# One-hot lookups turned round: the one-hot stationary, 512 table columns moving, seven tables and no pairs of tiles

## The reference

```python
e = jnp.stack([tbl_0[ids[:, 0]], ..., tbl_31[ids[:, 31]]], axis=1)      # (2048, 32, 256)
z = einsum('bnd,bmd->bnm', e, e)[:, iu, ju]                             # (2048, 496), i < j
h = concatenate([z, dense_ctx], axis=1)                                 # (2048, 512)
h = maximum(h @ W_top1 + b_top1, 0)                                     # 512
h = maximum(h @ W_top2 + b_top2, 0)                                     # 256
y = h @ W_top3                                                          # (2048, 1)
```

## Time and profile before

| | |
|---|---|
| median of 3 runs | 572.25 us (570.58 to 574.01) |
| the profiled execution | 570.71 us |
| its span | 568.9 us |
| TensorE matmul busy | 520.8 us (92%) |
| TensorE weight load busy | 472.5 us (83%) |
| ScalarE busy | 413.4 us (73%) |
| GpSimd busy | 405.4 us (71%) |
| VectorE busy | 129.8 us (23%) |

### The profile page before, as it was taken

The page is one execution under the profiler, slowest core; times in us unless marked ns, Lnnn a source line. Parts: engine busy times, 40 slices in busy tenths (PEclk is TensorE's granted clock), DMA queues, the critical chain, the costliest instruction groups (busy, mean ns, idle before and its releaser), DMA issues.

```text
span 568.9 us, 24720 instructions
## 1 busy us (share of the span) xinstructions
PE 520.8 (92%) x11291; PEld 472.5 (83%) x11291; DVE 129.8 (23%) x201; ACT 413.4 (73%) x743; POOL 405.4 (71%) x426
## 2 busy tenths in 40 slices
PE   0766999999999989999899999989999999999797
PEld 0656989999999989898789989989998999999655
DVE  1345031311304040312204040310404031220401
ACT  3968687878878778877678787867877887663502
POOL 6778777777777777777777777777777777777400
PEclk9977899999999999999999999989999999999999
DMA  8998744444344444444444444434444344433200
GB/s 188 258 237 213 200 120 122 116 125 121 114 130 116 126 121 114 120 125 114 121 126 117 125 119 118 119 113 130 117 124 122 115 115 122 108 112 108 76 3 2
DMA packets 32211, 71.00 MB, mean 125 GB/s; under 512 B 10382, under 2 KB 17438, under 8 KB 31358
## 3 DMA queue, kind: packets, MB, share of 16 engines
q0 software_dynamic: 20112, 54.95, 34.7%
q1 hardware_dynamic: 11996, 14.48, 10.5%
HBM read 69.39 MB, written 0.01 MB: 122 GB/s over the span
## 4 chain that ended last, share of the span: by engine, by line
PE 79%; DMA 8%; POOL 6%; issue 4%; ACT 2%; DVE 1%; DVEq 0%
PE look_ps L325 32%; PE gram_ps L343 18%; PE turn_ps L309 13%; DMA rows<-in_tbl,row_ids 7%; PE top_ps L368 7%; POOL rows L282 6%; PE top_ps L381 5%; PE turn_ps L388 2%; PE top_ps L358 1%; ACT area L474 1%; DVE turned L562 1%; ACT products L466 0%; DVE small L589 0%; ACT small L515 0%; PE turn_ps L368 0%
## 5 line engine op out<-in xcount | busy, mean ns | idle before, releaser
L282 POOL DMA_INDIRECT rows<-in_tbl,row_ids x419 | 404.7, 966 | 128.5 <-issue 115.8
L325 PE MATMUL look_ps<-one_hot,small 125*128 125x256 f32 (+1 forms) x1536 | 223.2, 295 | 0.5
L325 PEld LDWEIGHTS look_ps<-one_hot,small 125*128 125x128 f32 x1536 | 197.9, 196 | 3.3 <-issue 0.8
L309 PE MATMUL turn_ps<-ident,rows 128*128 128x128 f32 x838 | 127.5, 285 | 37.3 <-DMA rows<-in_tbl,row_ids 34.7
L507 ACT ACTIVATE one_hot<-ids_across,minus_rows 125x256 fp32r<-125x256 int32 (+1 forms) x384 | 155.5, 494 | 0.0
L309 PEld LDWEIGHTS turn_ps<-ident,rows 128*128 128x128 f32 x838 | 94.6, 144 | 48.1 <-DMA rows<-in_tbl,row_ids 25.0
L343 PEld LDWEIGHTS gram_ps<-turned 128*32 128x32 f32 x8192 | 92.2, 111 | 31.4 <-issue 11.4
L343 PE MATMUL gram_ps<-turned 128*32 128x31 f32 x8192 | 111.5, 199 | 5.6 <-DVE turned L562 3.6
L562 DVE COPY turned<-turn_ps 128x512 f32<-128x512 f32 (+1 forms) x130 | 84.1, 683 | 59.1 <-PE turn_ps L309 59.1
L443 ACT ACTIVATE turned<-turn_ps 128x512 f32<-128x512 f32 x80 | 49.4, 640 | 57.1 <-PE turn_ps L309 41.4
L510 ACT ACTIVATE one_hot<-one_hot 125x2048 fp32r<-125x2048 f32 (+1 forms) x48 | 89.3, 1860 | 1.5
(11 more groups left out here) (36 smaller groups left out, 98.5 us busy)
## 6 DMA issues: line engine op xcount, KB each, us to landing
rows<-in_tbl,row_ids POOLq DMA_INDIRECT x419
ids_across<-in_small_ids SPq DMA_DIRECT2D x45, 128.0 KB
area<-in_tbl SPq DMA_DIRECT2D x3, 896.0 KB
w_sb<-in_tbl SPq DMA_DIRECT2D x3, 896.0 KB
w_sb<-in_W_top SPq DMA_DIRECT2D x4, 256.0 KB
w_sb<-in_W_top SPq DMA_DIRECT2D x1, 512.0 KB
area<-in_tbl SPq DMA_DIRECT2D x3, 104.0 KB
w_sb<-in_tbl SPq DMA_DIRECT2D x3, 104.0 KB
```

What stands on the lines that cost most here:

```text
L282: pool.indirect_dma_start(out=rows[:, n % PLACES, j, :], out_offset=None, in_=tables[f], in_offset=bass.IndirectOffsetOnAxis(ap=row_ids[:, ...
L309: last = pe.transpose(turn_ps[n % RING][:, at:at + P], rows[:, n % PLACES, j, c * P:(c + 1) * P], ident[:, :])
L325: last = pe.matmul(look_ps[:, c * width:(c + 1) * width], small[:, f, r, part, c * P:(c + 1) * P], one_hot[n % 2][:, r, 0:width], start=(r ...
```

## The change

- Seven looked-up fields instead of six (three for tile 0 and five for tile 1, as the tables come in), each for one tile at a time.
- The one-hot (125 subrow values x 128 samples) is the stationary operand, and a subrow of the table moves: high and low part side by side, 512 columns into a whole PSUM bank. 8 matmuls a field and tile, 56 a tile. Each waits for its own one-hot and signals its own end.
- VectorE makes the one-hots, one `is_equal` for each subrow, in a ring of 12.
- The result is in rows: ScalarE copies the high half to `home_rows`, VectorE adds the low half. The looked-up fields are then units like the others, and are turned: 16 units a tile.
- `turn_ps` has three banks instead of four, `look_ps` two instead of one; the ring of gathered units has eight places instead of nine; three units are turned early instead of four. The eighth field, gathered, shares the unit of the last looked-up one.
- `ahead`, `place` and ScalarE's one-hots are gone. The ids come one tile at a time, through a ring of four.

```diff
-EVEN_FIELDS = [2, 4, 5]
-ODD_FIELDS = [6, 8, 9]
+SMALL_FIELDS = [2, 4, 5, 6, 8, 9, 14]
...
-    PLACES = 9
-    ACT_UNITS = [0, 2, 6, 9, 12]
-    RING = 4
-    LOOK_AFTER = [3, 7, 11]
-    SPLIT_AFTER = [1, 4, 7, 10, 13]
-    EARLY_AFTER = [3, 4, 5, 6]
-    TURN_FEATURES_AFTER = 6
-    LAYER1_AFTER = 9
+    LOOKED = [3, 5] + [SMALL] * (TILES - 2)
+    U = FIELDS // 2
+    HOMES = (SMALL + 1) // 2
+    PLACES = 8
+    ORDER_FIRST = [4, 5, 6, 7, 2, 3] + list(range(8, U)) + [1, 0]
+    ORDER = [4, 5, 6, 0, 1, 7, 2, 3] + list(range(8, U))
+    UNITS = [(tile, u) for tile in range(TILES) for u in (ORDER if tile else ORDER_FIRST)]
+    ACT_UNITS = [0, 1, 4, 6, 8, 10, 12, 14]
+    RING = 3
+    LOOK_AFTER = [4, 8, 12]
+    SPLIT_AFTER = [1, 4, 7, 10, 13, 15]
+    EARLY_AFTER = [4, 5, 6]
+    TURN_FEATURES_AFTER = 7
+    LAYER1_AFTER = 10
+    IDS_RING = 4
+    HOTS = 12
...
 # SP
-            for t in range(TILES):
-                if t + 2 in FIRST:
+            for n in range(FIRST[1] + IDS_RING, FIRST[2]):
+                load_ids(n)
+            for t in range(1, TILES):
+                load_dense(t)
+                if t + 1 < TILES:
                     for n in range(FIRST[t + 1], FIRST[t + 2]):
                         load_ids(n)
-                if t + 1 < TILES:
-                    load_dense(t + 1)
...
 # TensorE
-                for k in range(first, end):
-                    c, r, part = k // (2 * SUB), k // 2 % SUB, k % 2
-                    last = pe.matmul(look_ps[:, c * width:(c + 1) * width],
-                                     small[:, f, r, part, c * P:(c + 1) * P], one_hot[n % 2][:, r, 0:width],
-                                     start=(r == 0 and part == 0), stop=(r == SUB - 1 and part == 1))
+                for r in subrows:
+                    if r == 0 and n < FIRST[3]:
                         pe.wait_ge(low_ready, f + 1)
+                    if r == 0 and n >= 2:
+                        pe.wait_ge(looked_up, n - 1)
+                    pe.wait_ge(one_hot_made, n * SUB + r + 1)
+                    pe.matmul(look_ps[n % 2][:, :, :].rearrange("p k d -> p (k d)"), one_hot[:, (n * SUB + r) % HOTS, :],
+                              small[:, f, r, :, :].rearrange("p k d -> p (k d)"),
+                              start=(r == 0), stop=(r == SUB - 1)).then_inc(one_hot_used, 1)
...
+                made = (FIRST[t + 1] - FIRST[t]) * SUB
+                for at in range(made * k // (PARTS + 1), made * (k + 1) // (PARTS + 1)):
+                    look_up(FIRST[t] + at // SUB, [at % SUB])
...
 # ScalarE
+            def keep_high(n):
+                t, f = LOOKUPS[n]
+                act.wait_ge(one_hot_used, (n + 1) * SUB)
+                if t > 0:
+                    act.wait_ge(turn_done, UNITS.index((t - 1, f // 2)) + 1)
+                act.activation(home_rows[:, f // 2, f % 2, :], look_ps[n % 2][:, 0, :], ACT.Copy).then_inc(high_kept, 1)
...
+            for t in range(1, TILES):
+                for n in range(FIRST[t], FIRST[t + 1] - 1):
+                    keep_high(n)
+                for i in ACT_UNITS[:2]:
+                    keep_turned(t * U + i)
+                keep_high(FIRST[t + 1] - 1)
+                pick(t - 1)
+                for i in ACT_UNITS[2:4]:
+                    keep_turned(t * U + i)
+                keep_features(t - 1)
+                for i in ACT_UNITS[4:]:
+                    keep_turned(t * U + i)
+                keep_hidden1(t - 1)
...
 # VectorE
+            def make_one_hot(n, subrows):
+                if n >= len(LOOKUPS):
+                    return
+                dve.wait_ge(ids_across_in[n % IDS_RING], n_ids(n))
+                for r in subrows:
+                    at = n * SUB + r
+                    if at >= HOTS:
+                        dve.wait_ge(one_hot_used, at - HOTS + 1)
+                    dve.tensor_scalar(one_hot[:, at % HOTS, :], ids_across[0:SP, n % IDS_RING, :],
+                                      sub_row[:, r:r + 1], None, ALU.is_equal).then_inc(one_hot_made, 1)
+            def add_parts(n):
+                _, f = LOOKUPS[n]
+                home = home_rows[:, f // 2, f % 2, :]
+                dve.wait_ge(high_kept, n + 1)
+                dve.tensor_tensor(home, look_ps[n % 2][:, 1, :], home, ALU.add).then_inc(looked_up, 1)
...
             for t in range(TILES):
                 if t > 0:
                     unfold(t - 1)
+                    mine = [t * U + i for i in range(U) if i not in ACT_UNITS]
+                    for n in mine[:2]:
+                        keep_turned(n)
+                    add_parts(FIRST[t + 1] - 1)
+                    for n in mine[2:]:
+                        keep_turned(n)
+                    make_one_hot(FIRST[t + 1], range(SUB))
+                    make_one_hot(FIRST[t + 1] + 1, early)
+                if t + 1 < TILES:
+                    for n in range(FIRST[t + 1], FIRST[t + 2] - 1):
+                        make_one_hot(n + 1, late)
+                        if n < FIRST[t + 2] - 2:
+                            make_one_hot(n + 2, early)
+                        add_parts(n)
+                        if t > 0 and n == FIRST[t + 1]:
+                            last_layers(t - 1)
+                else:
                     last_layers(t - 1)
```

More of the change, by code:

```diff
@@ L83, in dlrm_tower @@
     STAGES = 2
[L84 to L100, removed]
+    IDS_RING = 4
+    HOTS = 12
+    LOOKUPS, FIRST = [], [0]
+    for tile in range(TILES):
+        LOOKUPS += [(tile, f) for f in range(LOOKED[tile])]
+        FIRST.append(len(LOOKUPS))
     ctx = ExitStack()
@@ L204, in n_dve_kept, with in_ring, place_of, last_in_place @@
             return sum(not by_act(m) for m in range(n + 1))
+        def in_ring(n):
+            return sum(u >= HOMES for _, u in UNITS[:n + 1])
+        def place_of(n):
+            return (in_ring(n) - 1) % PLACES
         def n_gathered(n):
-            return 16 * sum(len(UNITS[m][1]) for m in range(n % PLACES, n + 1, PLACES))
+            return 32 * ((in_ring(n) - 1) // PLACES + 1)
+        def last_in_place(n):
+            t, u = UNITS[n]
+            if u < HOMES:
+                return UNITS.index((t - 1, u)) if t > 0 else None
+            if in_ring(n) <= PLACES:
+                return None
+            return next(m for m in range(n) if UNITS[m][1] >= HOMES and in_ring(m) == in_ring(n) - PLACES)
+        def row_of(n, j):
+            u = UNITS[n][1]
+            return home_rows[:, u, j, :] if u < HOMES else rows[:, place_of(n), j, :]
         def n_ids(n):
@@ L275, in gather @@
             def gather(n):
[L276 to L277 removed]
+                t, u = UNITS[n]
+                fields = [f for f in (2 * u, 2 * u + 1) if not looked(t, f)]
+                if n == 0 or n == U:
                     pool.wait_ge(row_ids_in[t], 16)
[L279 to L281 removed]
+                if fields and last_in_place(n) is not None:
+                    pool.wait_ge(turn_done, last_in_place(n) + 1)
+                for f in fields:
                     pool.indirect_dma_start(
[L283 removed]
+                        out=row_of(n, f % 2), out_offset=None, in_=tables[f],
                         in_offset=bass.IndirectOffsetOnAxis(ap=row_ids[:, t, f:f + 1], axis=0),
[L285 removed]
+                    ).then_inc(home_gathered[f] if u < HOMES else gathered[place_of(n)], 16)
             pool.memset(ident[:, :], 0.0).then_inc(ident_zero, 1)
@@ L298, in turn @@
             def turn(n):
-                _, unit = UNITS[n]
-                pe.wait_ge(gathered[n % PLACES], n_gathered(n))
+                t, u = UNITS[n]
+                if u >= HOMES:
+                    pe.wait_ge(gathered[place_of(n)], n_gathered(n))
+                else:
+                    for f in (2 * u, 2 * u + 1):
+                        if looked(t, f):
+                            pe.wait_ge(looked_up, FIRST[t] + f + 1)
+                        else:
+                            pe.wait_ge(home_gathered[f], 16 * sum(not looked(m, f) for m in range(t + 1)))
                 if n >= RING:
@@ L306, in turn @@
                 for c in range(CHUNKS):
-                    for j in range(len(unit)):
-                        at = (c * len(unit) + j) * P
-                        last = pe.transpose(turn_ps[n % RING][:, at:at + P],
-                                            rows[:, n % PLACES, j, c * P:(c + 1) * P], ident[:, :])
+                    for j in range(2):
+                        at = (c * 2 + j) * P
+                        last = pe.transpose(turn_ps[n % RING][:, at:at + P], row_of(n, j)[:, c * P:(c + 1) * P],
+                                            ident[:, :])
@@ L390, in turn_all @@
             def turn_all(t):
-                for i in range(len(EARLY_AFTER), BEGIN[t + 1] - BEGIN[t]):
-                    turn(BEGIN[t] + i)
+                for i in range(len(EARLY_AFTER), U):
+                    turn(t * U + i)
                     if i == TURN_FEATURES_AFTER:
```

182 lines of the change are left out of this document (56 added, 126 removed).

## The result

The changed kernel takes 614.05 us (median of 5 runs, 610.89 to 615.28) against 572.25; the ratio is 1.0746, with a 95% interval of 1.0718 to 1.0773. The forecast was 602.5, range 578 to 635.

A forecast was written before the change was run, and what follows sets the result against it. Gathers at 32.5 us a tile were taken as the bound, TensorE close at 31.2. With TensorE's tile at 34.5, +31.4 + 0.5 - 1.6 = +30.3 us on 570.7 gave 601.0, plus 1.5 to the median: 602.5, range 578 to 635.

The forecast's parts named there:

- What bounds, and what takes over: Steady tile: gathers set it before (32.5 us against TensorE's 31.2); TensorE sets it after, at 34.5; chance 62%.
- The two waits: TensorE's turning stretch: 0.75 us for a ScalarE copy ahead of unit i=7, 1.15 us for the next tile's first one-hot.
- the walk: Step-by-step timing of the turning stretch, from the grams' end to the next grams: 14.75 us, 3.63 later than before.
- Unit i=7: Turning stretch, unit with the last lookup's field: starts at 4.25 instead of 3.5 us, a stall of 0.75.
- The products: Lookup matmuls on TensorE: 56 a tile of 512 columns at 0.240 us, 13.4 us, +0.3 a tile.
- The sum: Tile 31.2 + 3.6 - 0.3 = 34.5 us; in all +31.4, +0.5 and -1.6, so +30.3 us.
- The 0.216 quoted beside the sum: Lookup products: the Trainium skill's 216 ns for 512 columns, giving 12.1 us a tile and some 20 us less in all.
- The start: Startup: one more table +4.5 us, shorter first lookup -3, cheaper tile 1; together +0.5, within -4 to +5.
- The end: Behind the last layer-2 group: 0 forecast; the last tile's missing one-hot wait and six products were counted separately, -1.6.
- The rival: GpSimd becomes the bound as VectorE's one-hots hold up gathers: mild 32.8 us a tile, hidden; full 39, 665 total; chance 12%.
- Not slower: Lookup products: columns nearly free, 0.16 us each; gathers bound the tile at 31.25 us, 558 in all; chance 5%.

The follow-up runs named there:

- e1: Changed kernel with VectorE making the next tile's twelve one-hots ahead of its last two copies; ratio 1.0309 to the kernel before (904.71 us on that chip).
- g1: Changed kernel with one-hots ahead of VectorE's last copies, first subtraction ahead of the second lookup's one-hots, ScalarE's i=4 copy ahead of pick; 602.34 us, ratio 1.0528.
- e4_bench: Changed kernel plus 160 unread matmuls behind its last transpose, in bursts of 32; 512 columns 0.230 us each, 256 columns 0.120; no total time given.
- e2: Changed kernel with VectorE subtracting the first table ahead of the second lookup's one-hots in the startup; ratio 1.0318 to the kernel before (904.71 us).
- f4: Changed kernel without nine transposes a tile, so some values are not right; ratio 1.0056 to the kernel before (903.69 us).
- h2: f4 again: changed kernel without nine transposes a tile; ratio 1.0038 to the kernel before (901.82 us).
- f3: Changed kernel with the three edits of g1 and six looked-up fields instead of seven, nine places; ratio 1.0292 to the kernel before (903.69 us).
- h1: f3 without its startup edit: six looked-up fields, one-hots ahead, ScalarE's copy ahead of pick; ratio 1.0235 to the kernel before (901.82 us).

## Why the prediction was right, and where it was off

*What bounds, and what takes over.* Right: the gathers set the tile before, TensorE sets it after. The 14 tiles show no TensorE wait for rows, and GpSimd waits for TensorE. One reading behind it was wrong: of the 34.7 us that TensorE waited for rows before, 25.0 lie ahead of the first layer-2 group and only 9.8 in the 14 tiles. That the gathers were the bound is better seen on GpSimd: 356 gathers at 1.25 us are 445 of the 451.6 us of these tiles.

*The two waits.* Both came where the walk put them. The one-hot's is 1.12 us for 1.15 forecast, and e1's order took it away in e1 and in g1. Unit i=7 lost 0.46 for 0.75 forecast, and g1 shows that behind its wait stands another of the same length, for the pick. The stretch as a whole is 3.73 us longer for 3.63 forecast. Of the growth of the tile this is nearly all.

*The products.* This term was mis-sized. The sum had 56 x 0.240 = 13.4 us a tile, with 0.026 as an addend to each. By the bench and the timeline it is 0.230 each and about 0.2 for each burst. The 43 products of the gram stretch take 11.3 us, 0.263 each, where the sum had 10.3. Not all of the 1 us is lost, since the eight gram portions take 5.9 us in this tile and took 6.5 in that of the earlier trace rows (6.2 to 7.0 in the others); the sum did not count that, and why they are shorter was not looked into. What a tile takes outside the stretch from grams to grams is 35.08 - 14.85 = 20.23 us, before 31.20 - 11.12 = 20.08: +0.15 where the sum had -0.3. These 0.45 and the 0.1 of the walk are the tile's 35.1 instead of 34.5. So the tile came out as near as it did partly by luck: two errors of 1.0 and 0.6 us stand against each other. Over 14 tiles the sum had 31.4 - 1.6 = 29.8 us more, and it was 38.5: 8.7 of the 9.9 us by which the span was missed. (The median was missed by 11.6: the profiled execution lies 3.2 us below it, where 1.5 was added.) The 512-column price was worked out from layer-2 rows, where the addend was taken as one of the matmul. That it goes with the burst is what was missed. The 0.216 quoted beside the sum is 0.014 below the bench, the 0.240 of the sum 0.010 above.

*The start.* +0.5 forecast, +3.3 measured, the other 3 us. It stands at the first grams already (60.11, before 56.93). The sum counted bytes and left out a queue: VectorE's first one-hots of lookup 1 stand ahead of the first subtraction, and wait 12 us for ids that SP asked for behind four table transfers. That this holds up the third table by 8 us is shown by e2 and g1; what it costs the first grams came out between 0.1 and 4.2 us in three comparisons, so how much of the 3 us it explains stays open. That removing it wins time is refuted by all three, because the gathers, which subtractions hold up, are late next.

*The end.* 0 forecast, -1.7 measured: 0.9 is the spare matmul that the change takes out (two instructions of 0.454), which was not counted. The rest is in the same gram portions again: from the first behind the layer-2 group to the last spare matmuls it is 596.15 - 584.90 = 11.25 us, before 555.14 - 543.18 = 11.96.

*GpSimd and VectorE.* The rival was given 12%. Its mild form is what happened: gathers of 0.956 us in a tile instead of 0.95, against up to 3.05 for one that meets a two-operand subtraction. Gathers that overlap a one-hot take 0.960 on average and 1.07 at most, the others 0.946. One-hots had a median of 284 ns where 171 + 120 x 1.06 = 298 was forecast for the plain rate and 235 for double, so VectorE did not run them at double rate. The Trainium skill ("SBUF — State Buffer", section Who interferes with whom) ties the port lock of a one-input instruction to the two-port modes; the trace agrees in the main, no double rate and no gather held for the length of a one-hot, but the up to 0.12 us beside one-hots remain without a cause. The same section of the Trainium skill has it that an instruction with two SBUF inputs meets only GpSimd's reads of SBUF, and infers that descriptor generation goes on. Here each such subtraction, six in the kernel before and seven in the changed one, holds a gather up to its own end and 0.82 us beyond, and the measurement decides for such gathers. Each of them also takes its row numbers out of SBUF, so it may be this read that is held; no run separates the two.

*Not slower.* Refuted by e4_bench.

What stays open: that TensorE sets the tile was to be tested by leaving transposes out (f4, h2) and by the sixth table (f3, h1). Where those ran, something else set the time, so for this the traces of the changed kernel and g1 stand alone. g1 is a small test of it: a wait of 1.12 us taken off TensorE made the stretch 1.35 us and the mean tile 0.85 us shorter.

## What to carry to other kernels

Price a matmul that stands in short bursts by a burst and not by the matmul: here 0.230 us for each of 512 columns and another 0.2 for each change from grams to products and back. When work moves to another engine, walk that engine's queue for what now stands ahead of it: the order of two lines cost 1.1 us a tile, and it could be read before any run. And a wait that is taken away in a startup that several queues feed is only worth what the next late thing allows; here a gain of 4.2 us at the first grams stood beside a loss of 3.6 at the first layer-2 group.

## What the runs showed of the hardware

**A lack of instructions on TensorE.** In three of five series of runs the kernel before took 902 to 905 us instead of 572. The waits of e1 have, for grams alone:

```profile
PE gram_ps L362 <- issue: 122.0, 204, 1.8
```

and its timeline shows how it looks:

```profile
357.75 0.76 PE L362 MATMUL gram_ps<-turned 128*32 128x31 f32 x64
...
344.45 0.74 PE L362 MATMUL gram_ps<-turned 128*32 128x31 f32 x34
346.05 0.29 PE L362 MATMUL gram_ps<-turned 128*32 128x31 f32 x3 [0.85 <-issue]
...
347.48 0.34 PE L362 MATMUL gram_ps<-turned 128*32 128x31 f32 x4 [0.48 <-issue]
```

At 357.75 a portion of 64 gram matmuls takes 0.76 us; at 344.45 it stops after 34, and the rest comes a few at a time, after waits of mostly 0.4 to 1.2 us, while TensorE waits for nothing that the profile shows. It repeats in each tile at much the same places. The clock then adds to it. Windows of e1, columns as in the earlier trace rows:

```profile
325.00:333.00 8.00, 7.18 (x64) 7.03 (x63) 1.49 (x3) 2.00 (x4) 5.87 (x8) 1.00 0.32 78
337.50:356.00 18.50, 10.20 (x83) 7.71 (x84) 3.04 (x8) 2.32 (x6) 7.82 (x9) 0.50 0.26 75
357.75:365.00 7.25, 7.25 (x230) 5.44 (x233) 6.29 (x28) 0.77 (x2) 0.00 (x0) 1.00 0.06 14
```

The first waits of this tile, 0.8 to 1.2 us each from 332 us on, come at a granted clock of 1.00 (2.4 GHz); behind them it falls to 0.50 (1.2 GHz) for some 20 us. In the 18.5 us of the second line TensorE is busy for 10.2, and six products take 344.45 - 341.62 = 2.83 us. From 367 on portions stop again at the full clock. So the lack of instructions comes first here and the low clock behind it; the mean granted clock of e1 was 0.846, against 0.980 in the changed kernel. The small form is in the 572-us runs too: in g1 single gram portions come in two pieces, 1.1 us apart at the worst. What decides between the two was not found. The packets of the instruction queue were not slower: 0.99 us in the median in e1 and 0.98 in the changed kernel.

**A floor under a product.** With one load of 128 weight columns each, 128 moving columns cost 0.110 us and 256 columns 0.120, so between these two the number of matmuls counts and not their width; from 256 to 512 it is 0.110 more. It is not a floor of every matmul: 64 grams, with 32 weight columns and 31 moving ones, take 0.69 us, 0.011 each.

**Gathers beside VectorE.** A subtraction with two SBUF operands held the gather that met it until 0.82 us behind its own end, in 20 cases of 20 in three traces (1.89 to 3.05 us in place of 0.95).
